# One Trainium2 core: expert layers on gathered tokens, and four loads and stores moved across stage boundaries

## The reference

```python
logits = xt @ gate_w.T + gate_b
probs = jax.nn.sigmoid(logits)
w, idx = jax.lax.top_k(probs, TOP_K)                     # TOP_K = 2 of N_EXPERTS = 6
w = w / (jnp.sum(w, axis=-1, keepdims=True) + 1e-08)
ge = jnp.sum(jax.nn.one_hot(idx, N_EXPERTS, dtype=w.dtype) * w[..., None], axis=1)
y = jnp.zeros_like(xt)
for e in range(N_EXPERTS):
    h = jax.nn.silu(xt @ ew1[e].T) * (xt @ ew3[e].T)
    y = y + ge[:, e:e + 1] * (h @ ew2[e].T)
z = jax.nn.silu(xt @ fc1.T) * (xt @ fc2.T) @ fc3.T       # the shared expert
return (y + z).reshape(orig_shape)
```

## Time and profile before

| | us |
|---|---|
| median of 3 runs | 4684.81 |
| lowest, highest | 4669.04, 4697.14 |
| profiled execution | 4671.09 |
| its span | 4669.5 |
| PE busy | 4239.2 (91%) |
| DVE busy | 3004.6 (64%) |
| ACT busy | 2295.4 (49%) |
| POOL busy | 682.8 (15%) |

### The profile page before, as it was taken

The page is one execution under the profiler, slowest core; times in us unless marked ns, Lnnn a source line. Parts: engine busy times, 40 slices in busy tenths (PEclk is TensorE's granted clock), DMA queues, the critical chain, the costliest instruction groups (busy, mean ns, idle before and its releaser), DMA issues. The chain is left out here.

```text
span 4669.5 us, 79371 instructions
## 1 busy us (share of the span) xinstructions
PE 4239.2 (91%) x25648; PEld 2522.6 (54%) x25648; DVE 3004.6 (64%) x5513; ACT 2295.4 (49%) x4375; POOL 682.8 (15%) x698
## 2 busy tenths in 40 slices
PE   7999969999999999986999989639999999997688
PEld 6888743333333333324888855525656656654454
DVE  5556668888888888835656533746666666663432
ACT  3222317777777777761332222214656556655222
POOL 2232200000000000000233200532222222220000
PEclk9999979999999999987999999868999989998789
DMA  2000172323323322203000000476667667662401
GB/s 85 0 0 0 52 146 38 46 34 43 46 34 44 46 38 39 32 6 120 8 0 0 1 20 0 150 198 179 188 176 184 188 165 186 191 158 52 131 20 36
DMA packets 173944, 359.15 MB, mean 77 GB/s; under 512 B 40586, under 2 KB 104714, under 8 KB 156810
## 3 DMA queue, kind: packets, MB, share of 16 engines
q1 hardware_dynamic: 154634, 304.20, 28.5%
q0 software_dynamic: 18944, 50.35, 3.9%
HBM read 209.71 MB, written 152.06 MB: 77 GB/s over the span
## 5 line engine op out<-in xcount | busy, mean ns | idle before, releaser
L1314 DVE TENSOR_REDUCE full_tops<-psum 128x1 f32<-128x1024 f32 x1024 | 1206.2, 1218 | 184.0 <-PE psum L1218 184.0
L1271 ACT ACTIVATE full_probs<-psum 128x512 f32<-128x512 f32 x2048 | 1065.8, 602 | 299.2 <-PE psum L1190 295.1
L1781 ACT ACTIVATE causal_probs<-psum 128x512 f32<-128x512 f32 (+3 forms) x1280 | 640.2, 533 | 397.9 <-PE psum L1653 230.0
L1190 PE MATMUL psum<-full_q,full_k 49*128 49x512 f32 x2048 | 653.3, 475 | 23.2 <-ACT full_probs L1271 17.2
L1832 DVE TENSOR_REDUCE causal_tops<-psum 128x1 f32<-128x1024 f32 (+7 forms) x704 | 586.8, 857 | 112.6 <-PE psum L1704 112.6
L1190 PEld LDWEIGHTS psum<-full_q,full_k 49*128 49x128 f32 x2048 | 284.5, 186 | 605.8 <-ACT full_probs L1271 576.9
L1199 PE MATMUL psum<-full_probs,full_vh 128*32 128x512 f32 x4096 | 556.8, 616 | 0.7 <-ACT full_probs L1271 0.7
L1218 PE MATMUL psum<-full_k,full_q 48*128 48x512 f32 x2048 | 402.0, 458 | 51.4 <-DMA full_k<-qk_split 23.6
L1653 PE MATMUL psum<-causal_q,causal_k 49*128 49x512 f32 (+3 forms) x1280 | 407.7, 451 | 14.2 <-ACT causal_probs L1781 8.3
L1704 PE MATMUL psum<-causal_k,causal_q 48*128 48x512 f32 (+4 forms) x1152 | 325.3, 414 | 70.2 <-DVE causal_tops L1847 33.4
L274 POOL TENSOR_TENSOR moe_h_lo<-moe_h,moe_h_hi 128x512 fp32r<-128x512 f32 x224 | 290.3, 1296 | 661.2 <-ACT moe_h_hi L387 661.2
(11 more groups left out here) (190 smaller groups left out, 6070.7 us busy)
## 6 DMA issues: line engine op xcount, KB each, us to landing
causal_bias<-bias_tiles SPq DMA_DIRECT2D x32, 1280.0 KB, 6.3
band_scores<-xn POOLq DMA_DIRECT2D x256, 160.0 KB, 4.2
full_q<-qk_split SPq DMA_DIRECT2D x192, 128.0 KB, 6.3
full_k<-qk_split SPq DMA_DIRECT2D x192, 128.0 KB, 7.1
causal_q<-rot_parts SPq DMA_DIRECT2D x192, 128.0 KB, 5.4
causal_k<-rot_parts SPq DMA_DIRECT2D x192, 128.0 KB, 6.4
bias_tiles<-causal_skew_rows SPq DMA_DIRECT2D x32, 640.5 KB, 3.4
bias_tiles<-causal_skew_rows SPq DMA_DIRECT2D x32, 640.0 KB, 3.3
```

What stands on the lines that cost most here:

```text
L1190: nc.tensor.matmul(k.psum[:, b, :], k_sb[at, q, kt * P:(kt + 1) * P], q_sb[at, q, n * BLK:(n + 1) * BLK], start=True, stop=True).then_inc( ...
L1271: nc.scalar.activation(pT[:, kt % 4, n * BLK:(n + 1) * BLK], k.psum[:, bank(q, u), :], ACT.Exp).then_inc(p_ready, 1)
L1314: nc.vector.reduce_max(mx[:, q % 2, u // 2, u % 2:u % 2 + 1], src, AX_X).then_inc(m_free, 1)
L1781: nc.scalar.activation(dst, k.psum[:, bank(q, u), 0:(hi - lo) * P], ACT.Exp).then_inc(p_ready, 1)
```

## The change

The expert layer. The shared expert is still computed block by block (`v` 0 to 7). In the same passes the gate is computed with tokens on the partitions (20 matmuls a block, six columns each, no transpose back), `choose` ranks, `positions` counts on PE how many tokens before this one chose the same expert, `locate` turns that into two slot numbers per token, and POOL scatters the token numbers to the table `slot_tokens` in HBM, 8 indirect DMAs a block. The normalized rows go to HBM (`normed`). After the last block `schedule` works out a plan: 21 gathered blocks of 512 slots (16 full ones and up to 5 begun ones; the number is fixed), each with its expert. For each of them (`v` 8 to 28) SP loads the slots' token numbers, POOL gathers the rows of `normed` in 4 indirect DMAs, PE transposes, up and down run with that expert's weights (split anew for each block, from a slice that a register chooses), ACT copies the result out and SP stores it to `slot_outputs`. After all, POOL gathers for each of the 32 tiles its two rows of results (64 indirect DMAs), and DVE adds each, weighted, to X.

The other parts. X's four loads get a semaphore each and the stage ends when the identity matrix, now loaded second, is there. The buffers and constants of the heads stage are set up in the projection stage, and its first four heads are loaded there, after block 4's stores. Reciprocals of the first batch's sums are made at the end of the heads stage, those of the second beside the first loads of the output projection. The last gate layer stores each tile group of X as soon as it is updated, and `store_stage` is gone.

```diff
 # load_stage
-                sp.dma_start(k.X[:, i * n:(i + 1) * n, :], x_t[:, i * n:(i + 1) * n, :]).then_inc(s_in, 16)
-            sp.dma_start(k.ident[:, :], io["ident"][:, :]).then_inc(s_in, 16)
-            sp.wait_ge(s_in, 16 * 5)
+                sp.dma_start(k.X[:, i * n:(i + 1) * n, :], x_t[:, i * n:(i + 1) * n, :]).then_inc(k.loaded[i], 16)
+                if i == 0:
+                    sp.dma_start(k.ident[:, :], io["ident"][:, :]).then_inc(s_in, 16)
+            sp.wait_ge(s_in, 16)
 # moe_stage, SP
+                sp.wait_ge(plan_ready, 1)
+                sp.wait_ge(k.scattered, scattered_all())
+                for i in range(NX + 3):
+                    if i < NX:
+                        load_ids(i)
+                    if i >= 3:
+                        store(i - 3)
 # moe_stage, POOL
+                for v in range(NBLK - 2):
+                    rest(v + 1, 0)
+                    rest(v + 1, 1)
+                    scatter(v + 2)
...
+                gather(0)
+                gather(1)
+                rest(NBLK, 0)
+                gather(2)
+                rest(NBLK, 1)
+                for v in range(NBLK, NV - 1):
+                    rest(v + 1, 0)
+                    if v + 3 < NV:
+                        gather(v + 3 - NBLK)
+                    rest(v + 1, 1)
+                for r in range(2):
+                    pool.wait_ge(s_y[r], 16 * ((NX + 1 - r) // 2))
+                pool.wait_ge(back_ready, 1)
+                for g in range(TT):
+                    if g >= 8:
+                        pool.wait_ge(c_done, g - 7)
+                    for s, ring in enumerate((k.xn, ybuf)):
+                        pool.indirect_dma_start(
+                            out=ring[:, g % 8 // TB, g % TB, :], out_offset=None, in_=k.YS[:, :],
+                            in_offset=bass.IndirectOffsetOnAxis(ap=back[:, s, g:g + 1], axis=0)).then_inc(k.back[g % 8], 16)
 # moe_stage, PE
+                transpose(0)
+                gate(0)
+                positions(0)
+                transpose(1)
+                gate(1)
+                positions(1)
+                up(0, 0)
+                up(0, 1)
+                for v in range(NBLK - 2):
+                    transpose(v + 2)
+                    up(v + 1, 0)
+                    gate(v + 2)
+                    up(v + 1, 1)
+                    down(v, 0)
+                    positions(v + 2)
+                    down(v, 1)
...
+                for v in range(NBLK, NV):
+                    if v + 1 < NV:
+                        up(v + 1, 0)
+                    if v + 2 < NV:
+                        transpose(v + 2)
+                    if v + 1 < NV:
+                        up(v + 1, 1)
+                    down(v, 0)
+                    down(v, 1)
 # moe_stage, ACT
+                for v in range(NBLK, NV):
+                    if v + 1 < NV:
+                        hidden(v + 1, 0)
+                    if v + 2 < NV:
+                        upper_x(v + 2)
+                    if v + 1 < NV:
+                        hidden(v + 1, 1)
+                    out(v - NBLK, 0)
+                    out(v - NBLK, 1)
+                    if v + 3 < NV:
+                        split(v + 3 - NBLK)
 # moe_stage, DVE
+                for v in range(NBLK - 2):
+                    lower_x(v + 2)
+                    hidden(v + 1, 0)
+                    choose(v + 2)
+                    hidden(v + 1, 1)
+                    weigh(v + 2)
+                    update(v)
+                    locate(v + 2)
+                    if v + 3 < NBLK:
+                        apply(v + 3)
+                    if v + 4 < NBLK:
+                        stats(v + 4)
+                schedule()
...
+                for v in range(NBLK, NV):
+                    if v + 1 < NV:
+                        hidden(v + 1, 0)
+                    if v + 2 < NV:
+                        lower_x(v + 2)
+                    if v + 1 < NV:
+                        hidden(v + 1, 1)
+                    if v + 3 < NV:
+                        rest(v + 4 - NBLK)
 # qkv_full_stage, SP
-                with sp.Fori(0, NBLK) as n:
+                half = NBLK // NB + 1
+                with sp.Fori(0, half) as n:
+                    for u in range(NU):
+                        store(n, u)
+                sp.wait_ge(F.ones, 4)
+                for u in range(NU):
+                    sp.wait_ge(s_parts[u], 16 * (1 + half))
+                for q in range(4):
+                    load_full_head(k, sp, F, q, q)
+                with sp.Fori(half, NBLK) as n:
 # heads_full_stage, SP, at its end
+                sp.dma_start(rec[:, :], k.DD[0:H, :].rearrange("i (b c) -> (i b) c", b=QB)).then_inc(s_rec, 16)
+                sp.wait_ge(inverted, 1)
+                sp.dma_start(k.RD[0:H, :].rearrange("i (b c) -> (i b) c", b=QB), rec[:, :]).then_inc(s_rec, 16)
 # project_full_stage, SP
-            sp.dma_start(rec, k.DD.rearrange("i (b c) -> (i b) c", b=QB)).then_inc(s_rec, 16)
-            sp.wait_ge(s_rc, 1)
-            sp.dma_start(k.RD.rearrange("i (b c) -> (i b) c", b=QB), rec).then_inc(s_rec, 16)
-            sp.wait_ge(s_rec, 32)
+            sp.dma_start(rec, k.DD[H:2 * H, :].rearrange("i (b c) -> (i b) c", b=QB)).then_inc(s_rec, 16)
+            load(0, 0)
+            load(1, 1)
+            sp.wait_ge(s_rc, 1)
+            sp.dma_start(k.RD[H:2 * H, :].rearrange("i (b c) -> (i b) c", b=QB), rec).then_inc(s_rec, 16)
+            load(2, 0)
+            load(3, 1)
+            sp.wait_ge(s_rec, 32)
 # lstm_stage, SP, last run
+                        sp.wait_ge(x_done, 2 + n * NO + 2 * (t + 1))
+                        g = n * TB + t * (TT // NB)
+                        sp.dma_start(o_t[:, g:g + TB, :], k.X[:, g:g + TB, :]).then_inc(s_out, 16)
```

More of the change, by code:

```diff
@@ new lines, in moe_stage @@
+        more = sb("more", [P, E, NBLK])
+        nblk = sb("nblk", [P, E])
+        prior = sb("prior", [P, E, E])
+        first = sb("first", [P, E])
+        total = sb("total", [P, 1])
+        past = sb("past", [P, NX, E - 1])
+        base = sb("base", [P, NX, E - 1])
+        expert = sb("expert", [P, NX])
+        valid = sb("valid", [P, NX])
+        origin = sb("origin", [P, NX])
+        inner = sb("inner", [P, NX])
+        row = sb("row", [P, NX])
+        plan = sb("plan", [P, 2, NX], I32)
```

790 lines of the change are left out of this document (516 added, 274 removed).

## The result

| | us |
|---|---|
| the kernel before, median of 4 runs | 4690.98 (4669.04 to 4706.23) |
| the changed kernel, median of 4 runs | 4859.94 (4844.17 to 4866.63) |
| ratio, 95% interval | 1.0368 (1.0332 to 1.0405) |
| profiled execution of the changed kernel | 4866.63, span 4865.1 |

A forecast was written before the change was run, and what follows sets the result against it. PE was taken to bound the expert stages (98% busy). From the profiled 4671.1 us, +17 experts, +26 head loads, -9 reciprocals, -4 X, -9.5 output gave 4691.6, stated as 4690, no change; range 4560 to 4810.

The forecast's parts named there:

- opening: Expert stage start: two rounds of gate and positions, then the first shared unit's 24 matmuls; 49 us.
- six shared passes with the clock: Shared-block loop of the expert stage: six passes of 19.5 us, 117 us, plus 18 us for a lower clock.
- turn, restart, 20 periods, last block: Shared to gathered blocks: turn 26 us, slow restart 12.5, twenty gathered periods 224, last down, copy and store 9.
- combining: Expert stage end: 64 gathers in a row on POOL at 1.14 us, plus landing and last add; 76 us.
- I take a fifth, 3 us a pass: Shared passes: clock loss taken as a fifth, between bounds of nothing and all 15.2 us at 1.2 GHz.
- PE is 78% busy in a pass: Shared passes: the argument given against the rival that the clock falls.
- the gathered period: Gathered blocks: 11.2 us each, set by ACT and DVE hand-overs; PE needs 9.4 us, POOL 7.2.
- Early heads: Projection to heads: 48 early loads delay 12 stores, so heads begin at 681 instead of 653; +26 us.
- Reciprocals, output: Output projection: reciprocals' loads issued earlier, -9 us; program end: X stored block by block, -9.5 us.
- X in parts: Program start: identity loads second, but weights and tables still queue behind X; -4 us (-6 to 0).
- The clock falls: Rival, shared passes: all at 1.2 GHz costs 146 us more, 4838; half of it gives 4765; chance 0.20.
- DVE blocks POOL in the combining: Rival, combining: POOL stands still for each of 64 additions, 26 us a run, 4745; chance 0.09.

The follow-up runs named there:

- e5: Changed kernel with normalize and statistics ahead of the ranking on VectorE, plus the 20 gate matmuls spread over the second up; 4813.18 us, ratio 1.0258.
- e4: Changed kernel with a gathered block's four gathers put ahead of both rests of h on GpSimd; 4786.34 us, ratio 1.0176.
- e1: Changed kernel with the 48 loads of the first four heads moved back to the start of the heads stage; 4828.78 us, ratio 1.0272.
- e6: Changed kernel with the old expert stage and head loads back in the heads stage, leaving X in parts, reciprocals and output; 4649.74 us, ratio 0.9929.
- e7: e6 with only head 0's 12 loads issued in the projection stage, behind the last store on SP's queue; 4661.66 us, ratio 0.9940.

## Why the prediction was wrong

**What bounds the kernel, and the work saved.** Right: 27 units of 8.3 us went a run.

**Cost of the expert stage.** Wrong by 81 us in the first run, in these terms:

| term | predicted | measured |
|---|---|---|
| opening | 49 | 57.0 |
| six shared passes with the clock | 117 + 18 | 158.0 |
| turn, restart, 20 periods, last block | 26 + 12.5 + 224 + 9 | 311.2 |
| combining | 76 | 82.7, and 4.0 to the next stage |

The step that failed most plainly is "I take a fifth, 3 us a pass" for the clock. The pass at full clock was 19.5 us on paper, and the pass measured is 27.3, which leaves 7.8 to the clock, half of the 15.2 us that I had as the upper bound, at a pause (3.74 us) and a work list that were as worked out. I had weighed "PE is 78% busy in a pass" against it; e5 shows that argument empty. The opening ran at half clock up to 62 us, where the gate took 9.3 us and I had 7.5. It took 57.0 us in the first run and 51.8 in the second; the 5 us between them belong to X in parts, below.

The second, the largest of all in time, is the gathered period, 11.2 us on paper and 12.6 measured, 28 us a run. I added ACT's and DVE's hand-overs and compared POOL's total of 7.2 us with them, which is under the period, and dropped POOL. But the gathers' place in POOL's list, behind a rest that waits and ahead of one on which PE waits, cost what the total did not show; e4 removed it by order alone, 30 us a run.

The third is landing. I took 2.3 us for the scatters, the least that the earlier trace rows shows; 11.9 us passed between the end of the last scatter (236.0) and the end of SP's wait for them (247.9), and 10.0 in the second run of the stage (2505.4 to 2515.4). Those 9.6 us and the 28 make up 38 of the 40 us that the third row is off.

The indirect DMA itself: I took 1.14 us from bounds of 0.73 and 2.3. It holds POOL for 0.95 and the next starts 0.30 later; over 64 gathers that is 81 us for my 73. The nearest row was a good guide, the gap between two of them was missing from it.

**Early heads.** Right in mechanism and size: +26 predicted, +27.9 in the profiles, 29.8 by e1.
**Reciprocals, output.** -9 and -9.5 predicted; -8.4 (19.1 to 10.7) and -9.5 measured; e6 shows them together with the next.
**X in parts.** Right at -4, though the stage begins 8.8 us earlier: in e6, where the experts are the old ones, the first expert stage is 4.5 us longer than in the kernel before (530.9 against 526.4 from its first statistics to those of the next stage), since its tables and weights queue behind X, as the prediction had it. In the changed kernel ACT waits for the shared expert's weights until 18.6 with the copies of x behind it, and the first gate begins at 22.0, 14.2 us after the stage's start; in the second run it is 9.5.

**The rivals.** "The clock falls" was the case that came: its 4838, for passes wholly at the lower level, is nearest to 4859.94, but that nearness is luck. Half of the bound was lost to the clock in a pass (7.8 of 15.2 us), for which the rival had 4765; the passes lost 23 us a run beyond my allowance, not the 73 of the rival's upper case. The rest of the 81 us came from the gathered blocks, the turn and the opening. It had 0.20, and the range's upper end of 4810 left its own number out. "DVE blocks POOL in the combining" did not happen: the gathers take 0.95 us beside the additions as they do without them. The rule of the Trainium skill that I had beside it (SBUF — State Buffer, Who interferes with whom) is stated of a DVE instruction with two SBUF inputs beside a GpSimd one that reads SBUF. The additions are of that kind, and no gather was stretched (0.94 to 1.00 us each); whether issuing a gather is such a read no run here shows. The Trainium skill's page DMA: Bandwidth & Descriptors (Anatomy of one DMA) has 2.0 us fixed for a POOL-issued DMA, most of it latency. In the combining 2.8 us pass from the start of a gather (535.26) to the addition (538.09), 1.9 of them after POOL is free, which agrees; the scatters' 11.9 us do not.

## What to carry to other kernels

Work taken from a bound engine is worth its time only while that engine stays dense: cost every pause of some microseconds, and every stretch of narrow matmuls, at the lower clock as well, and expect nothing until all of them are gone. Where a helper engine gets DMAs to issue, its total is the wrong number to compare; look at what stands directly ahead of and behind each issue in its list, and put the issue into its idle time. Loads for a later stage belong behind the current stage's last store on a shared queue, or they take its buffers hostage; behind it they did no harm here, and no measurable good either (e7).

## What the runs showed of the hardware that I had not expected

An indirect DMA of 128 rows holds POOL for 0.95 us whether a row is 4 bytes (scatter, 0.96) or 1 KB (gather, 0.95), with 0.30 us between two. The last scatter took longer in each of the two runs, 1.88 and 1.44 us, and SP's wait for the scatters ended 11.9 and 10.0 us after it, while in the first run no packet is recorded in the last 9 of them; what takes that time no run here shows. Six-column float32 passes take 0.22 us at half clock and 0.12 at full, so they scale with the clock like wide ones, and yet it falls while they run. The same tail of the same instructions takes 73 to 89 us, by when the clock falls in it. And up to 62 us of the changed kernel the view gives a granted clock of 1.00 while 512-column matmuls start 0.43 us apart, which is the pace of 1.2 GHz: the trace has no clock entry there, and the spacing has to be read.

```profile
20.00:62.00 42.00, 31.23 (x125) 29.12 (x126) 19.11 (x86) 3.90 (x8) 12.02 (x12) 1.00 0.33 125
```
```profile
57.29 0.63 PE L486 MATMUL psum<-moe_x_lo,moe_w_hi 128*128 128x512 f32 x1
57.72 0.63 PE L486 MATMUL psum<-moe_x_hi,moe_w_lo 128*128 128x512 f32 x1
```
